# A chunked recurrent scan: products on single 32x32 blocks instead of block-diagonal 128x128 matrices

## The reference, cut to what matters

```python
def step(S, inp):
    rt, dt, kt, vt, at, bt = inp
    sa = jnp.einsum('bhij,bhj->bhi', S, at)
    S = S * dt[:, :, None, :] + sa[..., None] * bt[:, :, None, :] + vt[..., None] * kt[:, :, None, :]
    y = jnp.einsum('bhij,bhj->bhi', S, rt)
    return (S, y)
```

## Time and profile before

| | |
|---|---|
| median of the runs | 3923.72 us |
| profiled execution | 3921.58 us, its span 3919.7 us (1.9 us lie around the span) |
| TensorE matmul / weight load busy | 3082.4 us (79%) / 1734.7 us (44%), 16262 instructions each |
| VectorE busy | 2929.5 us (75%) |
| ScalarE busy | 1879.3 us (48%) |
| GpSimd busy | 1883.7 us (48%) |
| mean granted TensorE clock | 0.87 of 2.4 GHz |

### The profile page before, as it was taken

One profiled execution on the slowest core, in us unless ns is written; L12 is line 12 of the kernel. 1 busy time (PEld: TensorE's weight loads), 2 busy tenths in 40 slices (PEclk: granted clock), 3 DMA queues, 4 the chain that ended last, 5 costly groups with the idle time before them and its releaser, 6 DMA issues. The chain is left out here.

```text
span 3919.7 us, 46678 instructions
## 1 busy us (share of the span) xinstructions
PE 3082.4 (79%) x16262; PEld 1734.7 (44%) x16262; DVE 2929.5 (75%) x3862; ACT 1879.3 (48%) x2899; POOL 1883.7 (48%) x961
## 2 busy tenths in 40 slices
PE   8968888865638965898889988899888998666823
PEld 3457777753325742333434334343343443333512
DVE  4656666665711123999999999999999999996588
ACT  2433333222411114766677666677666775523434
POOL 0011111121221021779888888888888888861100
PEclk9967777777858986999999999999999999997966
DMA  1000000000032323344443444434444444331000
GB/s 42 0 7 1 0 0 0 0 6 19 0 109 87 117 79 102 129 149 140 162 140 133 148 141 161 143 130 158 141 152 143 135 153 140 129 118 35 1 20 22
DMA packets 120614, 342.23 MB, mean 87 GB/s; under 512 B 14763, under 2 KB 45698, under 8 KB 119714
## 3 DMA queue, kind: packets, MB, share of 16 engines
q1 hardware_dynamic: 114594, 332.01, 25.0%
q0 software_dynamic: 3072, 6.00, 0.8%
q10 hardware_dynamic: 2816, 2.62, 0.2%
HBM read 328.31 MB, written 14.68 MB: 88 GB/s over the span
## 5 line engine op out<-in xcount | busy, mean ns | idle before, releaser
L1950 POOL TENSOR_TENSOR mb_h<-mb_h,mb_BC 128x1024 f32<-128x1024 f32 x512 | 1212.8, 2389 | 406.8 <-DVE mb_h L2197 406.8
L2197 DVE TENSOR_TENSOR_SCAN mb_h<-mb_dA,mb_bx 128x1024 f32<-128x1024 f32 x512 | 1170.5, 2286 | 23.8 <-ACT mb_dA L2064 6.0
L2300 PE MATMUL mb_y<-mb_h,ident 128*128 128x512 f32 x2048 | 1000.0, 628 | 215.2 <-POOL mb_h L1950 213.4
L2064 ACT ACTIVATE mb_dA<-mb_delta,mb_A 128x511 f32<-128x511 f32 x1024 | 664.7, 713 | 415.3 <-DVE mb_h L2197 409.4
L2300 PEld LDWEIGHTS mb_y<-mb_h,ident 128*128 128x128 f32 x2048 | 387.7, 198 | 790.2 <-issue 415.3
L2193 DVE TENSOR_TENSOR mb_bx<-mb_du,mb_BC 128x1024 f32<-128x1024 f32 x512 | 630.3, 1231 | 42.7 <-DMA mb_BC<-mamba_BC 6.7
L744 POOL COPY rs_vs<-rw_v 128x256 f32 x16 | 9.8, 612 | 571.2 <-PE rs_p L1006 338.9
L245 PE MATMUL mb_p<-mb_xT,mb_in_w 128*128 128x512 f32 x512 | 238.1, 609 | 23.3 <-ACT mb_sz L1990 16.7
L245 PE MATMUL mb_p<-mb_upad,mb_convd 128*128 128x512 f32 x512 | 225.0, 592 | 0.8 <-ACT mb_upad L1978 0.8
L1674 DVE TENSOR_TENSOR me_h<-me_s,me_p 128x320 f32<-128x320 f32 x64 | 31.2, 488 | 242.6 <-ACT me_s L1651 242.6
L883 DVE TENSOR_TENSOR rs_PQX<-rs_p,rs_PQX 128x128 f32<-128x128 f32 x320 | 85.8, 290 | 114.8 <-PE rs_p L983 113.7
(11 more groups left out here) (439 smaller groups left out, 5554.2 us busy)
## 6 DMA issues: line engine op xcount, KB each, us to landing
mb_BC<-mamba_BC SPq DMA_DIRECT2D x256, 1024.0 KB, 5.2
me_W<-in_L_ffn_W SPq DMA_DIRECT2D x24, 1024.0 KB, 9.2
mb_in_w<-in_L_attn_in_proj_w SPq DMA_DIRECT2D x4, 1024.0 KB, 8.2
mb_convd<-in_mamba_taps SPq DMA_DIRECT2D x4, 1024.0 KB, 10.2
expert_rows<-me_zero SPq DMA_DIRECT2D x1, 2560.0 KB, 10.1
x<-in_x SPq DMA_DIRECT2D x4, 512.0 KB, 5.3
me_xe<-expert_rows SPq DMA_DIRECT2D x8, 256.0 KB, 10.7
expert_results<-me_oe ACTq DMA_DIRECT2D x8, 256.0 KB, 7.6
```

The costliest lines, as they stand in the source:

```text
L1950: tt(hk, hk, buffer(k, it)[:, 1, :, :], ALU.mult).then_inc(*pos(f"hc{k}{part}"))
L2064: i = av(dA[k % 2][:, c, s, 1:], delta[:, it % 2, mc, 1:], ACT.Exp, scale=A[:, MC * layer(it) + mc, n:n + 1])
L2197: nc.vector.tensor_tensor_scan(flat(h[k % NBUF][:, c, :, :]), flat(dA[k % 2][:, c, :, :]), flat(full(bx)), 0.0, ALU.mult, ALU.add).then_in ...
L2300: i = mm(ybank[c][:, :], m.ident[:, :], h[k % NBUF][:, c, s, :], start=False, stop=e == HALF - 1 and s == SU - 1)
```

## The change

The block-diagonal matrices, their mask and GpSimd's work on them go. Where a 128x128 product with a block-diagonal matrix stood, four products stand, one per chunk, each on its own rows s and, but for rp, its own output partitions s of the array. P and Q become `PQ[h]`, 128x(2x32); X gets its own tile. Round 3 of the doubling makes P alone and copies P alone. rp writes the four chunks to banks 4 to 7 and VectorE adds them in four instructions. The loops over tiles are Python loops: all 16 tiles are written out, and waits are on constants, without the increments of `passed`. The order of the work on TensorE, VectorE and ScalarE is the same.

```diff
-        Abd = [sb(f"rs_Abd{h}", [P, 4, P]) for h in range(H1)]
-        PQX = [sb(f"rs_PQX{h}", [P, 3 * P]) for h in range(H1)]
+        PQ = [sb(f"rs_PQ{h}", [P, 2, CH]) for h in range(H1)]
+        X = [sb(f"rs_X{h}", [P, 2, N1]) for h in range(H1)]
...
             def _(po):
-                with po.Fori(0, NT) as it:
-                    hold(po, m, pe.at("y1", it - 1))
+                for it in range(0, NT):
+                    po.wait_ge(*pe.at("y1", it - 1))
...
-                    for h in heads:
-                        po.wait_ge(*dve.at(f"ac{h}{LAST}", it))
-                        nc.gpsimd.tensor_tensor(
-                            Abd[h][:, :, :].rearrange("p m (q t) -> p m q t", q=NCH),
...
             def _(a):
-                        nc.scalar.activation(PQX[h][:, P:2 * P], bank[h][:, P:2 * P], ACT.Copy)
-                        nc.scalar.activation(PQX[h][:, 2 * P + N1:], bank[4 + h][:, N1:P], ACT.Copy).then_inc(*act(f"q{h}"))
+                        nc.scalar.activation(PQ[h][:, 1, :], bank[h][:, CH:2 * CH], ACT.Copy)
+                        nc.scalar.activation(X[h][:, 1, :], bank[4 + h][:, N1:P], ACT.Copy).then_inc(*act(f"q{h}"))
                     for k in range(4):
                         for h in heads:
+                            n = 2 if k < 3 else 1
                             a.wait_ge(*pe.at(f"n{h}{k}", it))
-                            nc.scalar.activation(PQX[h][:, 0:2 * P], bank[h][:, 0:2 * P], ACT.Copy).then_inc(*act(f"n{h}{k}"))
+                            nc.scalar.activation(PQ[h][:, 0:n, :], bank[h][:, 0:n * CH].rearrange("p (x t) -> p x t", x=n), ACT.Copy).then_inc(*act(f"n{h}{k}"))
...
             def _(v):
                             if l == 0:
-                                hold(v, m, pe.at(f"lv{h}", it))
-                                hold(v, m, pool.at(f"bd{h}", it - 1))
+                                v.wait_ge(*pe.at(f"lv{h}", it))
                             else:
-                                hold(v, m, dve.at(f"ac{h}{l - 1}", it))
+                                v.wait_ge(*dve.at(f"ac{h}{l - 1}", it))
...
-                    nc.vector.tensor_tensor(RT[:, :, :], bank[4][:, 0:W2].rearrange("p (c n) -> p c n", c=DC), rt_of(it), ALU.add).then_inc(*dve("rp"))
+                    for q in range(NCH):
+                        s = slice(CH * q, CH * q + CH)
+                        i = nc.vector.tensor_tensor(RT[:, :, s], bank[4 + q][:, 0:DC * CH].rearrange("p (c n) -> p c n", c=DC), rt_of(it)[:, :, s], ALU.add)
+                    i.then_inc(*dve("rp"))
...
             def _(t):
+                quads = [slice(CH * q, CH * q + CH) for q in range(NCH)]
+                def chunks(h, kind):
+                    return Ac[h][:, kind[0], kind[1], :]
...
                     for h in heads:
-                        t.wait_ge(*pool.at(f"bd{h}", it))
-                        nc.tensor.transpose(bank[h][:, P:2 * P], Abd[h][:, BA, :], m.ident[:, :])
-                        mm(bank[4 + h][:, N1:P], Abd[h][:, KA, :], vs[:, h * N1:(h + 1) * N1], start=True, stop=True).then_inc(*pe(f"q{h}"))
+                        t.wait_ge(*dve.at(f"ac{h}{LAST}", it))
+                        for s in quads:
+                            mm(bank[h][s, CH:2 * CH], chunks(h, BA)[s, :], m.ident[s, s], start=True, stop=True)
+                        for s in quads:
+                            i = mm(bank[4 + h][s, N1:P], chunks(h, KA)[s, :], vs[s, h * N1:(h + 1) * N1], start=True, stop=True)
+                        i.then_inc(*pe(f"q{h}"))
...
-                            if k < 4:
-                                mm(bank[h][:, P:2 * P], Pk, PQX[h][:, P:2 * P], start=True, stop=True)
-                                mm(bank[h][:, 0:P], PQX[h][:, P:2 * P], Pk, start=True, stop=True)
-                            mm(bank[4 + h][:, 0:P], Pk, PQX[h][:, 2 * P:3 * P], start=True, stop=True).then_inc(*pe(f"n{h}{k}"))
+                            if k < 3:
+                                for s in quads:
+                                    mm(bank[h][s, CH:2 * CH], Pk[s, :], Qk[s, :], start=True, stop=True)
+                            if k < 4:
+                                for s in quads:
+                                    mm(bank[h][s, 0:CH], Qk[s, :], Pk[s, :], start=True, stop=True)
+                            for s in quads:
+                                i = mm(bank[4 + h][s, 0:P], Pk[s, :], X[h][s, :, :].rearrange("p x i -> p (x i)"), start=True, stop=True)
+                            i.then_inc(*pe(f"n{h}{k}"))
...
-                        i = mm(bank[4][po:po + N1, hp * P:(hp + 1) * P], W[h], Abd[h][:, BR, :], start=True, stop=True)
+                        for q, s in enumerate(quads):
+                            i = mm(bank[4 + q][po:po + N1, hp * CH:hp * CH + CH], W[h][s, :], chunks(h, BR)[s, :], start=True, stop=True)
...
                     for h in heads:
-                        mm(y_out(h), Abd[h][:, BR, :], U[h], start=False, stop=False)
-                        i = mm(y_out(h), Abd[h][:, KR, :], vs[:, h * N1:(h + 1) * N1], start=False, stop=False)
+                        for s in quads:
+                            mm(y_out(h)[s, :], chunks(h, BR)[s, :], U[h][s, :], start=False, stop=False)
+                        for s in quads:
+                            i = mm(y_out(h)[s, :], chunks(h, KR)[s, :], vs[s, h * N1:(h + 1) * N1], start=False, stop=False)
```

More of the change, by code:

```diff
@@ L183, in shape_constants @@
         "level_masks": np.ascontiguousarray(level.astype(np.uint32)),
-        "block_mask": np.repeat((np.arange(P)[:, None] // 32 == np.arange(4)[None]).astype(np.float32)[:, :, None], 32, 2),
         "chunk_reset": np.tile((np.arange(256) % 32 != 0).astype(np.float32), (P, 1)),
@@ L698, in rwkv_scan @@
         AT, BT, KT = range(3)
-        BA, BR, KA, KR = range(4)
+        BA, BR, KA, KR = ((x, y) for x in range(2) for y in range(2))
         heads = range(H1)
@@ L708, in rwkv_scan @@
         act = signal("scalar", "tm " + each("q") + " ".join(f"n{h}{k}" for k in range(4) for h in heads) + " nn")
-        pool = signal("pool", "vs " + each("xa") + each("bd"))
+        pool = signal("pool", "vs " + each("xa"))
         dvf, acf = signal("vector_f", "cum dif left right base end"), signal("scalar_f", "ep em")
@@ L733, in _ @@
             def _(sp):
-                for dst, src in ((levelmask, g["level_masks"]), (blockmask, g["block_mask"]), (reset, g["chunk_reset"]),
+                for dst, src in ((levelmask, g["level_masks"]), (reset, g["chunk_reset"]),
                                  (eye64, g["eye_twice"]), (bound, g["carry_bound"])):
@@ L795, in _ @@
                 body(0, state=False)
-                with a.Fori(1, NT - 1) as it:
+                for it in range(1, NT - 1):
                     body(it)
@@ L804, in _ @@
                 stt = nc.vector.scalar_tensor_tensor
[L805 removed]
+                v.wait_ge(masks_in, 64)
                 nc.vector.memset(left[:, :, 0, 0:1], 0.0)
@@ L881, in body @@
                             v.wait_ge(*pe.at(f"n{h}{k}", it))
-                            X = PQX[h][:, 2 * P:3 * P]
-                            nc.vector.tensor_tensor(X, bank[4 + h][:, 0:P], X, ALU.add).then_inc(*dve(f"x{h}{k}"))
+                            nc.vector.tensor_tensor(X[h][:, :, :], bank[4 + h][:, 0:P].rearrange("p (x i) -> p x i", x=2), X[h][:, :, :], ALU.add).then_inc(*dve(f"x{h}{k}"))
                         if following and k == 0:
@@ L905, in _ @@
                 body(0, state=False)
-                with v.Fori(1, NT - 1) as it:
+                for it in range(1, NT - 1):
                     body(it)
@@ L916, in _ @@
                 begin(t, pe, pes)
-                W = [PQX[h][:, 2 * P:2 * P + N1] for h in heads]
-                U = [PQX[h][:, 2 * P + N1:3 * P] for h in heads]
+                W = [X[h][:, 0, :] for h in heads]
+                U = [X[h][:, 1, :] for h in heads]
+                quads = [slice(CH * q, CH * q + CH) for q in range(NCH)]
+                def chunks(h, kind):
+                    return Ac[h][:, kind[0], kind[1], :]
                 half = [(h // 2, N1 * (h % 2)) for h in heads]
@@ L924, in state_step @@
                 def state_step(it, q):
-                    hold(t, m, dvs.at(f"s{q - 1}", it) if q else dvs.at("carry", it - 1))
+                    t.wait_ge(*dvs.at(f"s{q - 1}", it) if q else dvs.at("carry", it - 1))
                     for h in heads:
@@ L949, in body @@
                 def body(it, state=True):
-                    hold(t, m, dvf.at("end", it))
-                    hold(t, m, dve.at("mt", it - 1))
-                    hold(t, m, act.at("nn", it - 1))
+                    t.wait_ge(*dvf.at("end", it))
+                    t.wait_ge(*dve.at("mt", it - 1))
+                    t.wait_ge(*act.at("nn", it - 1))
                     for x in range(3):
@@ L960, in body @@
                         if h == 2:
-                            hold(t, m, act.at("tm", it))
```

(13 more changed lines are left out.)

17 lines of the change are left out of this document (6 added, 11 removed).

## The result

| | before | after |
|---|---|---|
| median of the runs | 3922.4 us (4 runs, 3917.3 to 3923.8) | 3862.5 us (4 runs, 3856.4 to 3877.5) |
| profiled execution | 3921.58 us | 3865.45 us |
| from the transposes of tile 1 to those of tile 15 | 528.20 us, 37.73 a tile | 473.76 us, 33.84 a tile |
| TensorE matmul records | 16262 | 22726 |
| mean granted clock | 0.870 | 0.861 |

The ratio is 0.9855, with a 95% interval from 0.9825 to 0.9886: faster by 1.5%, which is 60 us between the medians and 56 between the profiled executions. The forecast was 3886, its range 3840 to 3924.

What follows compares the result with a forecast made beforehand. It took the scan as one chain that changes engines. Per tile 1.9 + 1.0 + 0.1 - 0.1 - 0.3 = 2.6 us, 39 us over 15 tiles, less 3 us for new code, gave 3886 us, range 3840 to 3924.

Steps and rivals of the forecast that it cites:

- two of the signs by which it called itself wrong: Wrong if heads exceed 0.8 us, clock 1.00 shows in the doubling, "issue" exceeds 1 us or the period 37 us.
- The price of a small product: Four diagonal blocks run together: a group of four costs 0.053, 0.107 or 0.213 us for 32, 64 or 128 columns at 0.50.
- The rival of blocks one by one, or in pairs: q and doubling: diagonal blocks don't all run together; about 4430 us one by one, 4078 in pairs; chance 0.09.
- (a): Tile start to round 0: q starts at 10.2 us and takes 1.3; round 0 starts at 11.5, 1.9 us less.
- (b): Round 0 of the doubling: 0.64 us per head, 2.56 us for four heads, 1.0 us less.
- (c): Rounds 1 and 2: the decay, exponentials and copies chain still bounds, TensorE hides under it with little to spare; 0.1 us less.
- The clock: Granted TensorE clock, taken as 0.50 for the whole scan.
- (d): Rounds 3 and 4 at clock 0.50: 4.44 us against 4.36 now, 0.1 us more.
- (e): rp to the next transposes: L888 becomes four instructions, 0.3 us more; mn and y1 lie beside VectorE.
- (f): Tiles written out: new code costs 0.2 us a tile, 3 us in all; bounds nothing and 3.4 us a tile.
- the clock is granted after all: Rival, doubling: round 0 saves 0.6 more, rounds 3 and 4 take 2.5 us; 2.5 us more a tile, 3848; chance 0.20.
- The rival of supply: An instruction-supply gap recurs every 196 matmul records: 0.8 us a tile worse, 3934 us; chance 0.05.

Runs made afterwards that it cites:

- kernel 4: The changed kernel with 128 redundant one-column 32x32 products added to mn in each tile: 4195.9 us, ratio 1.0696.
- kernel 2: The kernel before with its tile loops written out and plain waits, block-diagonal products kept: 3901.9 us, ratio 0.9948.
- kernel 3: The changed kernel with VectorE's decay of the next tile and ScalarE's exponentials moved to the head of the tile: 3860.4 us, ratio 0.9845.
- kernel 5: The changed kernel with P's products with Q and X joined into one of 160 columns in rounds 0 to 2: 3869.1 us, ratio 0.9855.
- kernels 7 and 8: 7: kernel 3 with the product for X cut in two, 3937.5 us; 8: changed kernel with early decay, joined products, TensorE's list in a loop, 3938.5 us.
- kernel 1: The changed kernel's small products, but with the tile loops and held waits left as in the kernel before: 3970.7 us, ratio 1.0117.

## Why the prediction was right, and where it was not

The sign, the place (inside the tiles, nothing else) and the time in its range were right. But two of the signs by which it called itself wrong came true: clock 1.00 in the doubling, and over 1 us of "issue" a tile. It had the tile 2.6 us shorter, less 0.2 for new code; measured are 3.9 us: 1.25 ahead of q, 1.3 in q and round 0, 1.35 in rounds 1 to 4, and nothing behind them. By its steps:

- **The price of a small product** was right: 0.64 us from head to head in round 0. The rival of blocks one by one, or in pairs, is out. Four row groups write one bank within 0.64 us a head, where one by one it would be 2.55; the rule of the Trainium skill, "TensorEngine Tiling (Array Packing)", section "Gotcha 1: PSUM Pressure", isn't borne out here (the four blocks write different partitions of the bank). At clock 1.00 24 records start in 0.34 us, 14 ns a record; nor is the floor of about 25 ns (the Trainium skill, "TensorE: Matmul & The Clock Gate", section "Wait — 56ns, not 53.3ns?") borne out across tiles of the array. Within one tile of the array kernel 4's records are 31 ns or more apart, which agrees with it.
- **(a)** 9.92 + 1.35 for 10.2 + 1.3 us: right, with TensorE's 1.84 us a head as the new bound. It counted the gain there from the plain waits, and kernel 2 bears that out.
- **(b)** 2.56 us, as forecast, at clock 0.50.
- **(c)** 6.21 us in this tile for 6.3: right as a time. The spare was said to be little, and TensorE's own work fell from 5.66 to 3.74 us instead, so the cover seemed wide. It wasn't: under the chain lay the supply, and the chain's removal alone (kernel 3) uncovered it.
- **The clock, and with it (d), failed.** The step was "I take 0.50 for the whole scan", from the levels, which do stay at 0.50. Over tiles 1 to 14 the granted clock was 0.52 in q and round 0, and 0.83, 0.88, 0.96 and 1.00 in rounds 1 to 4. From the last addition of round 2 to that of round 4 it is 3.28 us for 3.85 before, where (d) forecast slightly more than before. Counted from round 0's to round 4's it is 8.90 for 10.25: 1.35 us a tile gained where (c) and (d) cancelled, and most of what the forecast missed.
- **(e)** was forecast at 0.3 worse; the stretch is 9.85 us for 9.83, means over the tiles. Four instructions for L888 cost 0.62 us until the last ends, for 0.42 of the one; it is lost in the rest. mn takes 3.85 us, not 5.1, with a clock of 0.73 over the stretch for the 0.50 assumed, and stays beside VectorE.
- **(f) was mis-sized.** It was "0.2 us a tile", from the single gap of tile 0; it measured 1.8 us a tile of TensorE's idle time, beside the 0.4 before q that are a wait for ScalarE. Its argument, records a us, was the right quantity, but counted over the wrong stretch: the levels of the earlier trace rows come behind a wait, in which instructions can be fetched ahead (that is argued, not tested), and the doubling has none. At clock 1.00 a head wants 48 instructions in 0.34 us, 140 a us, against the 75 that arrive. The two errors are linked: at 0.50 it would have wanted 75 a us, just what comes. So the higher clock gave back less than the rival said (3848 us for "the clock is granted after all"), and the result, 3862, lies between it and the forecast. Part of the closeness is that offset, not insight.
- **The rival of supply** had the right mechanism and the wrong sign for this kernel: 1.8 us a tile, partly in stretches where something else was late too, as kernel 5 shows, whose tile is no shorter with a third of the gaps. It decides in kernels 7 and 8, slower than before by 0.3%, and has a part in kernel 1, slower by 1.2%.

In the first 250 us the transposes of tile 0 start between 244.6 and 254.0 us over these kernels (before 245.2, after 247.6). That was not followed up.

## What to carry to other kernels

Cutting block-diagonal products into tiles of the array multiplies the instructions, so work out two rates for each dense stretch: columns at either clock, and instructions a microsecond against what new code is supplied at. A stretch with two bounds shows no gain from removing either; when an edit that should help gives nothing, keep it, remove what is late next, and time both together. Before giving work to an idle GpSimd, list what VectorE does with two SBUF operands, and what it copies within SBUF, at that time.

## What the runs showed of the hardware

- New code reaches TensorE at some 75 instructions a us (128, 192 and 256 instructions in 1.70 to 1.84, 2.59 and 3.44 to 3.87 us), in transfers of 16 KB, 256 instructions each; a hole is up to 2.4 us long and ends 1.2 to 1.6 us behind a transfer. With 566 matmul records in a tile of 36.5 us new code leaves no hole (kernel 2). A loop of 566 matmul records and their weight loads runs without being fetched again, one of 874 does not.
- Four 32x32 tiles on the diagonal of the array work together and write one PSUM bank: 24 records in 0.64 us at clock 0.50 and in 0.34 at 1.00, no more than their columns' price.
- Products on one and the same tile of the array follow at 0.031 us even with one column, at clock 1.00, and at 0.053 at 0.50.
- Beside a GpSimd multiplication from SBUF, a VectorE multiplication of two SBUF operands takes 2.22 us for 0.41, and a copy of 8 elements 2.31 for 0.16; additions with an operand in PSUM keep their 0.29.
